# Graph network edge stage: a table chunk moved behind the first units, and DMA issues reordered

## The chip, the cores and the metric

The kernel runs on one core of a Trainium2 chip. The metric is the device time of one execution in microseconds (us). An instruction stream runs on each engine: TensorE (PE, with its weight loads PEld), VectorE (DVE), ScalarE (ACT), GpSimd (POOL) and SyncE (SP, which only waits and issues DMAs).

## The reference, cut to what matters

1250 nodes with 512 features, 40000 edges sorted by destination, two layers. The first layer takes nearly all the time. It works edge by edge:

```
h        = relu(layernorm(x))
pre      = [h[src], h[dst], edge_attr] @ W1 + b1        # 40000 x 1088 @ 1088 x 512
messages = mish(mish(pre) @ W2 + b2)                     # 40000 x 512 @ 512 x 512
agg      = segment_sum(messages, dst)                    # 1250 x 512
u        = mish([h, agg] @ W3 + b3)
x        = x + layernorm(h + u @ W4 + b4) * gamma + beta
```

The second layer is a low-rank product, `h @ U * s @ Vt`, and a sum over the neighbours with the weight of each edge, then bias, relu and residual. The kernel turns that sum into a product with a weighted adjacency matrix M of 1250 x 1250, which it builds in the edge stage of layer one, while it passes over the edges anyway.

## The kernel before, in words

**Prologue.** `h` is transposed and split in a high and a low part (nTh, nTl), so that three products in fast arithmetic give one of full precision. Two tables are made from it in ten chunks of 128 nodes: A = h @ W1[0:512], stored to A_tab, and B = h @ W1[512:1024] + b1, stored as a high and a low half to Bh_tab and Bl_tab. A chunk of B is 12 matmuls on PE (line 723) into one of three banks pB, then on DVE `store_b`: the bias is added (L464), the high half cast (L466), the low half subtracted (L468); SP stores both (`save_b`, L805 and L806). B's ten chunks are the last PE work of the prologue; DVE does `store_b` of them between the first preparations of the edge stage.

**Edge stage.** The edges come in 79 groups of 512. A group has four units: in the first half of the work a unit is a quarter of the 512 hidden features for all 512 edges, in the second half it is a quarter of the edges. Five programs, one for each engine, are written by hand as a loop over slots. In slot s, PE does the first product of unit s+5 (`gathered`: four transposes of gathered rows, L1137; `products`: two matmuls, L1145 and L1147), the second product of unit s (`msg`, 12 matmuls, L1158) and two small ones for M (L1168, L1169); after every fourth slot (s mod 4 = 2) eight matmuls sum the messages of a group by destination (L1181). Units 0 to 3 are done ahead of the slots in four banks (bp0, bp1, pm, bs); the last of them, bs, shares its memory with bank 2 of pB. ACT does exponentials and logarithms of mish (L1217 to L1223 for the first half, L1237 to L1245 for the second); DVE does the square (`square`, L1321), the product and the cast (`pre`, L1331 and L1337), the message (L1344), the bias copy (`bias`, L1350) and the one-hot matrices. Each wait is on a semaphore, and each engine takes its instructions in the written order.

**POOL.** In slot s it subtracts the low half of unit s+4 (`low`, hTl, L1063), and issues DMAs: four indirect gathers for each group (xg, from A_tab, tiles t = 0 to 3, L1050), two that add the summed messages into agg_tab (`accumulate`, L1077) and two that add 128 x 160 pieces into M_tab (`adjacency`, halves 0 and 1, L1088). The tables GATHER_AHEAD and ADJ_LAG say in which slot of four each is issued. Before, tile 0 of a group comes in a slot with s mod 4 = 2, tile 1 with 3, tile 2 with 0 and tile 3 with 1, two slots ahead of its use by PE (s mod 4 = 3 in `gathered`, unit s+5, j = 0, which waits for all four). Each add waits for the landing of the one before it.

**SP.** It loads, per group, the source indices (idx, `indices`, L970), the edge features (ea, L978), the destinations (db, L983), the rows of B in the group's window (`window_rows`, L957 and L958, which needs the products of the group two before) and a copy within the core (`window_copy`, L962). Between the loads of groups 2 and 3 it writes zeros over M_tab in ten DMAs of 640 KB (`zero_m`, L370). POOL's first add into M waits until all ten have landed (semaphore q_zlate, "e_zlate" in the listings).

Of the kernel before, what the change touches and what calls it, by code (L numbers as in the profile page):

```python
# [26 lines left out]
P = 128  # L27
# [188 lines left out]
def gnn_two_layers(nc, x, src_idx, dst_rows, src_cols, dst_cols, eaT, ew_cols, W1, b1, W2, b2, W3, b3, W4, b4,  # L216
# [39 lines left out]
    with ctx:  # L256
# [128 lines left out]
        with st:  # L385
# [70 lines left out]
            def store_b(e, c):  # L456
# [7 lines left out]
                e.tensor_tensor(tb[i][:], pB[i][:, :], b1b[:], ALU.add).then_inc(c_tb, 1)  # L464
                e.wait_ge(c_tb, 3 * c + 1)
                e.tensor_copy(tbh[i][:], tb[i][:]).then_inc(c_tb, 1)  # L466
                e.wait_ge(c_tb, 3 * c + 2)
                e.tensor_tensor(tbl[i][:], tb[i][:], tbh[i][:], ALU.subtract).then_inc(c_tb, 1)  # L468
# [238 lines left out]

            @prologue.on("tensor")
            def _(e):
                e.wait_ge(c_g.sem, 4)  # L710

                def table(c, half, bank):

                    n = 0
                    for a, w in ((nTh, w1h), (nTl, w1h), (nTh, w1l)):
                        if c == 0 and a is nTh and w is w1h:
                            e.wait_ge(*((c_w1h, 1) if half else (c_v.sem, v["w1h"])))
                        if c == 0 and w is w1l:
                            e.wait_ge(c_v.sem, v["w1l", half])
                        if half == 0 and a is nTl:  # L720
                            e.wait_ge(c_lo, c + 1)
                        for k in range(KC):
                            last = e.matmul(bank[:, :], a[:, k, c * P:(c + 1) * P], w[:, half * KC + k, :],
                                            start=n == 0, stop=n == 3 * KC - 1)
                            n += 1
                    return last

                def table_a(c):

                    e.wait_ge(c_hi, c + 1)  # L730
                    if c >= 2:
                        e.wait_ge(c_ta, c - 1)
                    table(c, 0, pA[c % 2]).then_inc(c_A, 1)

                def table_b(c):

                    if c >= TB:
                        e.wait_ge(c_tb, 3 * (c - TB) + 1)
                    table(c, 1, pB[c % TB]).then_inc(c_B, 1)
# [13 lines left out]
                for c in range(NCH):  # L753
                    table_b(c)
# [84 lines left out]
def edge_narrow(work, scope, sem, k):  # L839
# [9 lines left out]
    b_stored, store_b, save_b, q_b2, c_ta, c_tb = (  # L849
        k[n] for n in ("b_stored", "store_b", "save_b", "q_b2", "c_ta", "c_tb"))  # L850
# [26 lines left out]
    with st:  # L877
# [87 lines left out]
        def _(e):  # L965
# [49 lines left out]
            for i in range(3):  # L1015
                zero_m(e, i, q_zlate)
# [1473 lines left out]
```

## Time and profile before

| | us |
|---|---|
| median of 3 runs (1515.99 to 1518.47) | 1516.13 |
| the profiled execution | 1518.77 |
| its span, first to last instruction | 1517.1 |
| PE busy | 1489.8 |
| DVE busy | 1411.0 |
| ACT busy | 1302.0 |
| POOL busy | 1079.7 |

How to read a profile's rows. In a timeline a row has the start from the span's first instruction, the duration, the engine (with q for its queue's own instructions), the line, the operation, output<-inputs, the shape, how many instructions are merged in the row, and in brackets the idle time of the engine ahead of it with what ended that. In the windows view a row gives the busy time and the number of instructions of each engine in a stretch, then the granted clock of TensorE (1.00 is 2.4 GHz, 0.50 is 1.2 GHz), the busy share of the DMA engines and the rate they moved. In the waits view a row says who waited for what, total us, times, longest.

### The profile page before, as it was taken

The numbers are of one execution on the slowest core, as the hardware profiler recorded it, in microseconds if no ns is written. First come the engines' busy times: TensorE is split into PE (matmuls) and PEld (weight loads), VectorE is DVE, ScalarE is ACT, GpSimd is POOL, SyncE is SP. The second block draws the span as 40 slices with busy tenths as digits, with TensorE's granted clock in tenths as the row PEclk, the third lists the DMA queues.
The fourth block names the chain that finished last, engine by engine and source line by source line (L and its number), as shares of the span: only waits on it lengthen the run. The fifth ranks groups of instructions, "written<-read, shape, count | busy, mean of one in ns | idle before, by whom it ended". The sixth has DMA issues, their size and how long they took to land.

```text
span 1517.1 us, 33370 instructions
## 1 busy us (share of the span) xinstructions
PE 1489.8 (98%) x7862; PEld 1167.1 (77%) x7862; DVE 1411.0 (93%) x2920; ACT 1302.0 (86%) x2510; POOL 1079.7 (71%) x978
## 2 busy tenths in 40 slices
PE   7989999999999999999999999999999999999998
PEld 6767777777777777777777777777777777777885
DVE  7888999999999999999999999999999999996676
ACT  5088999999999999999999999999999999996562
POOL 1266888888888888887888888888878888863320
PEclk9999999999999999999999999999999999999999
DMA  8784555455455545444554545454455555554773
GB/s 288 269 280 107 122 123 125 112 131 116 118 122 123 122 115 129 116 118 118 125 118 115 125 123 121 118 125 118 115 123 123 123 117 126 115 135 102 176 166 148
DMA packets 124756, 205.10 MB, mean 135 GB/s; under 512 B 31641, under 2 KB 57369, under 8 KB 124720
## 3 DMA queue, kind: packets, MB, share of 16 engines
q0 software_dynamic: 58528, 112.91, 34.5%
q1 hardware_dynamic: 65840, 91.24, 19.3%
q10 hardware_dynamic: 352, 0.52, 0.1%
q8 instruction: 16, 0.26, 0.1%
q14 instruction: 20, 0.16, 0.0%
HBM read 151.60 MB, written 42.75 MB: 128 GB/s over the span
## 4 chain that ended last, share of the span: by engine, by line
PE 82%; DVE 5%; issue 4%; DMA 4%; POOL 2%; ACT 1%; POOLq 1%; DVEq 0%; SPq 0%; ACTq 0%
PE bm L1158 49%; PE bp L1137 7%; PE bp L1145 5%; PE bs L1181 4%; PE bp L1147 4%; DMA xg<-A_tab,idx 2%; PE pm L1169 2%; PE po L2146 2%; PE pu L336 2%; PE pu L2124 2%; PE pm L1168 1%; POOL hTl L1063 1%; DMA A_tab<-ta 1%; DVE bm L1350 1%; PE pu L2191 1%
## 5 line engine op out<-in xcount | busy, mean ns | idle before, releaser
L1063 POOL TENSOR_TENSOR hTl<-tp,hTh 128x512 fp32r<-128x512 f32 (+1 forms) x314 | 413.0, 1315 | 204.0 <-DVE khl L1357 203.2
L1158 PE MATMUL bm<-W2h,hTh 128*128 128x512 f32 x1252 | 498.3, 398 | 1.2 <-DVE bm L1350 0.8
L1158 PE MATMUL bm<-W2l,hTh 128*128 128x512 f32 x1252 | 496.7, 397 | 0.0
L1158 PE MATMUL bm<-W2h,hTl 128*128 128x512 f32 x1252 | 494.6, 395 | 0.0
L1050 POOL DMA_INDIRECT xg<-A_tab,idx x305 | 321.6, 1054 | 65.3 <-issue 37.7
L1158 PEld LDWEIGHTS bm<-W2h,hTh 128*128 128x128 f32 x1252 | 235.4, 188 | 71.0 <-DVE bm L1350 15.8
L1158 PEld LDWEIGHTS bm<-W2l,hTh 128*128 128x128 f32 x1252 | 235.4, 188 | 57.4
L1158 PEld LDWEIGHTS bm<-W2h,hTl 128*128 128x128 f32 x1252 | 235.5, 188 | 53.7
L1217 ACT ACTIVATE rp<-bp 128x512 f32<-128x512 f32 (+1 forms) x314 | 183.7, 585 | 107.1 <-PE bp L1147 77.3
L1321 DVE SCALAR_TENSOR_TENSOR rp<-rp 128x512 f32<-128x512 f32 (+1 forms) x314 | 214.8, 684 | 36.9 <-ACT rp L1217 17.5
L1331 DVE SCALAR_TENSOR_TENSOR tp<-rp,bp 128x512 f32<-128x512 f32 (+1 forms) x314 | 211.6, 674 | 4.7 <-ACT rp L1223 2.4
L1344 DVE SCALAR_TENSOR_TENSOR tm<-rm,bm 128x512 f32<-128x512 f32 x313 | 210.1, 671 | 3.4 <-ACT rm L1245 3.4
L1350 DVE COPY bm<-b2b 128x512 f32<-128x512 f32 x309 | 210.2, 680 | 0.0
L1220 ACT ACTIVATE rp<-rp 128x512 f32<-128x512 f32 (+1 forms) x314 | 195.5, 623 | 8.8 <-DVE rp L1321 3.0
L1241 ACT ACTIVATE rm<-rm 128x512 f32<-128x512 f32 x313 | 198.0, 633 | 5.0
L1245 ACT ACTIVATE rm<-rm 128x512 f32<-128x512 f32 x313 | 195.2, 624 | 0.1
L1243 ACT ACTIVATE rm<-rm 128x512 f32<-128x512 f32 x313 | 195.1, 623 | 0.1
L1223 ACT ACTIVATE rp<-rp 128x512 f32<-128x512 f32 (+1 forms) x314 | 194.1, 618 | 0.1
L1237 ACT ACTIVATE rm<-bm 128x512 f32<-128x512 f32 x313 | 185.5, 593 | 1.9 <-DVE tm L1344 1.8
L1137 PEld LDWEIGHTS bp<-ident_r,xg 128*128 128x128 f32 (+1 forms) x1244 | 123.8, 141 | 75.3 <-issue 38.0
L1077 POOL DMA_DIRECT2D agg_tab<-ev x157 | 157.1, 1001 | 25.8 <-DMA agg_tab<-ev 16.0
L1088 POOL DMA_DIRECT2D M_tab<-mev x157 | 164.3, 1047 | 10.4 <-issue 9.5
(248 smaller groups left out, 2306.6 us busy)
## 6 DMA issues: line engine op xcount, KB each, us to landing
ea<-in_eaT SPq DMA_DIRECT2D x156, 128.0 KB
M_tab<-mev POOLq DMA_DIRECT2D x157, 80.0 KB, 5.7
agg_tab<-ev POOLq DMA_DIRECT2D x157, 64.0 KB, 2.5
db<-in_dst_rows SPq DMA_DIRECT2D x78, 128.0 KB
M<-M SPq DMA_DIRECT2D x76, 128.0 KB
M_tab<-zero SPq DMA_DIRECT2D x10, 640.0 KB
xg<-A_tab,idx POOLq DMA_INDIRECT x313
eaW<-Bh_tab SPq DMA_DIRECT2D x77, 64.0 KB
```

What stands on the lines that cost most here:

```text
L1050: e.indirect_dma_start(out=xg[p][0:r, t, :].bitcast(F32), out_offset=None, in_=A_d, in_offset=bass.IndirectOffsetOnAxis(ap=idx[p][0:r, t:t ...
L1063: e.tensor_tensor(hTl[p][:, j, 0:w], pick(u, start_t, tp)[:, 0:w], hTh[p][:, j, 0:w], ALU.subtract)\
L1137: e.matmul(bank[:, t * P:t * P + r].bitcast(F32R), xg[p][0:r, t, j * P:(j + 1) * P], ident_r[0:r, 0:r], start=t == 0, stop=False, is_trans ...
L1158: last = e.matmul(bank[0:r, :], a[p][:, c, j * P:j * P + r], w[:, c, :], start=False, stop=c == KC - 1 and w is W2l, skip_group_check=True)
L1220: e.activation(t, t, ACT.Ln, bias=1.0, scale=0.5 / (SQ * SQ)).then_inc(a_pre, 1)
L1241: e.activation(t, t, ACT.Square, bias=SQ, scale=SQ).then_inc(a_msg, 1)
L1243: e.activation(t, t, ACT.Ln, bias=0.5, scale=0.5 / (SQ * SQ)).then_inc(a_msg, 1)
L1245: e.activation(t, t, ACT.Exp, scale=-1.0).then_inc(a_msg, 1)
L1321: e.scalar_tensor_tensor(t, t, 2.0 * SQ, t, ALU.add, ALU.mult).then_inc(v_sq, 1)
L1331: e.scalar_tensor_tensor(t, pick(u, start_r, rp)[:, 0:w], 1.0, pick(u, start_bank, bp)[:, 0:w], ALU.subtract, ALU.mult).then_inc(v_pre, 2 ...
L1344: e.scalar_tensor_tensor(tm[m.const % MBUF][0:r, :], rm[m.const % 2][0:r, :], 1.0, bm[m.j][0:r, :], ALU.subtract, ALU.mult).then_inc(v_msg, 1)
L1350: e.tensor_copy(bm[m.j][:, :], b2b[:]).then_inc(v_bias, 1)
```

## The change

1. B's tenth chunk (c = 9) leaves the prologue on PE and stands behind the products of units 0 to 3 (`table_b(e, NCH - 1)`). PE's wait for the add of chunk 8 (bank bs) now stands only ahead of unit 3.
2. On DVE, `store_b` of that chunk goes behind the four `pre` steps of units 0 to 3. Its sum is written to ta[0] instead of tb[0] (after a wait for the stores of A), and the square of unit 4 stands between its add and its cast. The bias copies into banks 2 and 3 follow it instead of standing among the first squares. The wait for all stores of B moves from the start of the slots to message 2.
3. POOL waits for c_B = 10 (the tenth chunk's matmuls) ahead of the low halves of units 1 to 3.
4. POOL issues tile 3 of a gather behind tile 2, in the same slot (s mod 4 = 0). Half 1 of the adds into M moves from there to the next slot (s mod 4 = 1), behind the add into agg_tab. The two first adds into M both stand in slot 9 (before: slots 6 and 8), one behind the other.
5. SP: the ten zero DMAs of M move behind the loads of group 3 (three of them) and behind the window rows of group 4 (seven).

```diff
@@ store_b
-                e.tensor_tensor(tb[i][:], pB[i][:, :], b1b[:], ALU.add).then_inc(c_tb, 1)
+                total = tb[i] if c < NCH - 1 else ta[0]
+                if c == NCH - 1:
+                    a_stored(e)
+                e.tensor_tensor(total[:], pB[i][:, :], b1b[:], ALU.add).then_inc(c_tb, 1)
+                if between:
+                    between()
...
@@ tables
-    GATHER_AHEAD = {2: (10, (0,)), 3: (9, (1,)), 0: (8, (2,)), 1: (7, (3,))}
+    GATHER_AHEAD = {2: (10, (0,)), 3: (9, (1,)), 0: (8, (2, 3))}
...
-    ADJ_LAG = {2: (6, 0), 0: (8, 1)}
+    ADJ_LAG = {2: (6, 0), 1: (9, 1)}
@@ SP
             b_stored(e)
             window_rows(At(None, 8))
+            window_copy(At(None, 8))
+            loads(At(None, 12))
             for i in range(3):
                 zero_m(e, i, q_zlate)
-            window_copy(At(None, 8))
-            indices(At(None, 12))
-            for i in range(3, 5):
+            indices(At(None, 16))
+            features(At(None, 16))
+            targets(At(None, 16))
+            window_rows(At(None, 16))
+            for i in range(3, NCH):
                 zero_m(e, i, q_zlate)
...
+            window_copy(At(None, 16))
+            loads(At(None, 20))
@@ PE
-            e.wait_ge(c_tb, 3 * (NCH - 2) + 1)
             for j in range(SUB):
+                if j == SUB - 1:
+                    e.wait_ge(c_tb, 3 * (NCH - 2) + 1)
                 gathered(At(None, j))
             for j in range(SUB):
                 products(At(None, j))
+            table_b(e, NCH - 1)
@@ POOL, low and adjacency
                 if first(u) and j:
                     e.wait_ge(a_high, j)
+                    e.wait_ge(c_B, NCH)
...
+                    u = s + -lag
+                    if u.has(4 * FULL) and not (half == 0 and u.reg is None and u.const == 0):
+                        if half == 1 and u.reg is None and u.const == 0:
                             e.wait_ge(q_zlate, 16 * NCH)
-                        adjacency(s + -lag, half)
+                            adjacency(u, 0)
+                        adjacency(u, half)
@@ DVE
-            square(u[0])
-            square(u[1])
-            biases(2)
-            square(u[2])
-            biases(3)
+            for j in range(3):
+                square(u[j])
             pre(u[0], 0)
             pre(u[0], 1)
             square(u[3])
             for j in range(1, SUB):
                 pre(u[j], 0)
-            square(u[4])
-            b_stored(e)
+            store_b(e, NCH - 1, lambda: square(u[4]))
+            biases(2)
+            biases(3)
```

The same work stays in the other branch of the program (general graphs), which these inputs do not take.

PE at the end of the prologue, before: chunk 9 into pB, then units 0 to 3 (bp, bp, pm, bs), and then unit 4 (names in brackets are the semaphores waited for).

```order
L723 MATMUL pB<-w1h,nTh 128x512 [waits c_tb]
L723 MATMUL pB<-w1h,nTh 128x512 x3
L723 MATMUL pB<-w1h,nTl 128x512 x4
L723 MATMUL pB<-w1l,nTh 128x512 x4
L138 TENSOR_LOAD wide_i [waits c_v]
L138 ISA x2
L139 COMPARE_AND_BRANCH
L1137 MATMUL bp<-ident_r,xg 128x128 [waits e_ga0,c_tb]
```

The same place after:

```order
L138 TENSOR_LOAD wide_i [waits c_v]
L138 ISA x2
L139 COMPARE_AND_BRANCH
L1142 MATMUL bp<-ident_r,xg 128x128 [waits e_ga0]
L1142 MATMUL bp<-ident_r,xg 128x128 x7
L1142 MATMUL pm<-ident_r,xg 128x128 x4
L1142 MATMUL bs<-ident_r,xg 128x128 [waits c_tb]
L1142 MATMUL bs<-ident_r,xg 128x128 x3
L1150 MATMUL bp<-M_0,eaW_0 128x512 [waits e_ealow,e_win0]
```

The wait for chunk 8's add has moved to the fourth unit, and chunk 9's matmuls stand behind the eight that begin with L1150 (there as L724).

POOL in the loop, before, the two slots s mod 4 = 0 and 1:

```order
L1063 TENSOR_TENSOR hTl<-tp,hTh 128x512 [waits v_adj]
L1050 DMA xg<-A_tab,idx 128x512
L1082 ISA
L1082 TENSOR_LOAD base_i
L1082 ISA x2
L953 REGISTER_ALU
L1088 ISA [waits e_adjq]
L1088 DMA M_tab<-mev 128x160
L1062 REGISTER_ALU
L1063 TENSOR_TENSOR hTl<-tp,hTh 128x512 [waits v_adj]
L1050 DMA xg<-A_tab,idx 128x512
```

The same two slots after:

```order
L1067 TENSOR_TENSOR hTl<-tp,hTh 128x512 [waits v_adj]
L1053 DMA xg<-A_tab,idx 128x512 x2
L1066 REGISTER_ALU
L1067 TENSOR_TENSOR hTl<-tp,hTh 128x512 [waits v_adj]
L1072 ISA
L1072 TENSOR_LOAD base_i
L1072 ISA x2
L1077 ISA
L958 ISA [waits e_ev]
L1081 ISA [waits e_acc]
L1081 DMA agg_tab<-ev 32x512
```

Tile 3 stands one subtraction and one add earlier; the add into agg_tab (which waits for DVE's e_ev) now follows the subtraction directly, and the add into M comes behind it.

SP after, from the loads of group 4 on (M_0, eaW_0: even groups):

```order
L975 DMA idx<-in_src_idx 128x4 [waits e_ga0]
L983 DMA ea<-in_eaT 64x512 [waits e_ealow]
L983 DMA ea<-in_eaT 64x512
L988 DMA db<-in_dst_rows 64x512
L993 TENSOR_LOAD base_i
L993 ISA x2
L962 ISA [waits e_pre]
L962 DMA eaW_0<-Bh_tab 32x512
L963 DMA eaW_0<-Bl_tab 32x512
L370 DMA M_tab<-zero 512x1x320 x7
L967 DMA M_0<-M_0 64x512 [waits e_prep]
```

The copy of group 4 (L967) and all of group 5's loads stand behind seven zero DMAs, which themselves wait for unit 11's products (e_pre).

## Rows read from the trace of the kernel before

**Rows 1.** The page: busy time (share) and instructions of each engine.

```profile
PE 1489.8 (98%) x7862; PEld 1167.1 (77%) x7862; DVE 1411.0 (93%) x2920; ACT 1302.0 (86%) x2510; POOL 1079.7 (71%) x978
```

**Rows 2.** Timeline of PE in the loop: sums by destination, one transpose group behind.

```profile
132.27 1.06 PE L1181 MATMUL bs<-tm,oh 128*32 128x512 f32 x8
...
715.57 0.52 PE L1137 MATMUL bp<-ident_r,xg 128*128 128x128 f32 x4 [0.31 <-DMA xg<-A_tab,idx]
...
780.82 1.06 PE L1181 MATMUL bs<-tm,oh 128*32 128x512 f32 x8
...
797.37 1.06 PE L1181 MATMUL bs<-tm,oh 128*32 128x512 f32 x8
...
1362.37 1.06 PE L1181 MATMUL bs<-tm,oh 128*32 128x512 f32 x8
```

**Rows 3.** Waits between 132 and 1362 us: total us, times, longest.

```profile
PE bp L1137 <- DMA xg<-A_tab,idx: 3.4, 7, 0.6
```

**Rows 4.** Timeline of POOL in the loop.

```profile
711.90 1.07 POOL L1050 DMA_INDIRECT xg<-A_tab,idx  x1 [0.16 <-DVE ev L1372]
...
725.98 1.01 POOL L1088 DMA_DIRECT2D M_tab<-mev  x1
...
728.49 1.06 POOL L1050 DMA_INDIRECT xg<-A_tab,idx  x1 [0.16 <-issue]
...
731.72 1.29 POOL L1063 TENSOR_TENSOR hTl<-tp,hTh 128x512 fp32r<-128x512 f32 x1 [1.21 <-DVE khl L1357]
```

**Rows 5.** Timelines at the start of the edge stage: ACT's queue, then PE.

```profile
69.88 0.37 ACTq L958 DMA_DIRECT2D eaW<-Bl_tab  x1
...
74.64 0.46 PE L1145 MATMUL bp<-M,eaW 128*128 128x512 f32 x1
```

**Rows 6.** The same stretch: DVE, POOL, DVE, PE.

```profile
74.24 0.43 DVE L466 CAST tbh<-tb 128x512 fp32r<-128x512 f32 x1
...
77.22 0.69 DVE L1408 COPY bm<-b2b 128x512 f32<-128x512 f32 x1
...
83.44 3.01 POOL L1063 TENSOR_TENSOR hTl<-tm,hTh 128x512 fp32r<-128x512 f32 x2
...
84.61 0.69 DVE L1321 SCALAR_TENSOR_TENSOR rp<-rp 128x512 f32<-128x512 f32 x1 [1.18 <-ACT rp L1217]
...
86.86 0.69 DVE L1331 SCALAR_TENSOR_TENSOR tp<-rp,bp 128x512 f32<-128x512 f32 x1 [1.56 <-ACT rp L1223]
...
87.60 0.53 PE L1137 MATMUL bp<-ident_r,xg 128*128 128x128 f32 x4
```

**Rows 7.** The page's DMA issues: count, KB each, median us to landing.

```profile
M_tab<-mev POOLq DMA_DIRECT2D x157, 80.0 KB, 5.7
agg_tab<-ev POOLq DMA_DIRECT2D x157, 64.0 KB, 2.5
```

**Rows 8.** Timelines of PE and POOL around group 3's first unit.

```profile
108.05 0.49 PE L1137 MATMUL bp<-ident_r,xg 128*128 128x128 f32 x4
...
112.00 1.07 PE L1181 MATMUL bs<-tm,oh 128*32 128x512 f32 x8
115.23 0.64 PE L1137 MATMUL bp<-ident_r,xg 128*128 128x128 f32 x4 [2.16 <-DMA xg<-A_tab,idx]
...
120.62 0.49 PE L1137 MATMUL bp<-ident_r,xg 128*128 128x128 f32 x4
...
109.11 0.97 POOL L1050 DMA_INDIRECT xg<-A_tab,idx  x1 [0.15 <-issue]
```

**Rows 9.** Windows: busy time by engine, granted clock, DMA share, GB/s.

```profile
104.00:108.00 4.00, 4.00 (x23) 3.34 (x22) 4.00 (x9) 3.97 (x8) 2.62 (x3) 1.00 1.05 362
...
115.50:118.70 3.20, 3.20 (x10) 2.61 (x10) 1.12 (x3) 1.75 (x4) 0.38 (x1) 0.50 0.44 93
```

**Rows 10.** Timeline of POOL at the end of the edge stage.

```profile
1389.21 0.88 POOL L1088 DMA_DIRECT2D M_tab<-mev  x1 [0.43 <-issue]
...
1392.69 0.88 POOL L1088 DMA_DIRECT2D M_tab<-mev  x1 [0.84 <-DMA M_tab<-mev]
```

More of the change, by code:

```diff
@@ L454, in b_stored, with store_b @@
                     e.wait_ge(q_sb[i], 32 * len(range(i, n, TB)))
-            def store_b(e, c):
+            def store_b(e, c, between=None):
                 i = c % TB
@@ L706, in _, with table, table_b @@
                 store_a(e, 9)
+            def table(e, c, half, bank):
+                n = 0
+                for a, w in ((nTh, w1h), (nTl, w1h), (nTh, w1l)):
+                    if c == 0 and a is nTh and w is w1h:
+                        e.wait_ge(*((c_w1h, 1) if half else (c_v.sem, v["w1h"])))
+                    if c == 0 and w is w1l:
+                        e.wait_ge(c_v.sem, v["w1l", half])
+                    if half == 0 and a is nTl:
+                        e.wait_ge(c_lo, c + 1)
+                    for k in range(KC):
+                        last = e.matmul(bank[:, :], a[:, k, c * P:(c + 1) * P], w[:, half * KC + k, :],
+                                        start=n == 0, stop=n == 3 * KC - 1)
+                        n += 1
+                return last
+            def table_b(e, c):
+                if c >= TB:
+                    e.wait_ge(c_tb, 3 * (c - TB) + 1)
+                table(e, c, 1, pB[c % TB]).then_inc(c_B, 1)
             @prologue.on("tensor")
@@ L710, in _ @@
                 e.wait_ge(c_g.sem, 4)
[L712 to L726, printed above, removed]
                 def table_a(c):
@@ L732, in table_a @@
                         e.wait_ge(c_ta, c - 1)
[L733 to L739, printed above, removed]
+                    table(e, c, 0, pA[c % 2]).then_inc(c_A, 1)
                 for c in range(NCH):
@@ L752, in _ @@
                 table_a(NCH - 1)
-                for c in range(NCH):
-                    table_b(c)
+                for c in range(NCH - 1):
+                    table_b(e, c)
             @prologue.on("sync")
@@ L1112, in step @@
                     lag, half = ADJ_LAG[s.j]
-                    if (s + -lag).has(4 * FULL):
-                        if half == 0 and s.reg is None and s.const == lag:
-                            e.wait_ge(q_z, 16 * ZERO_DMAS)
+                    u = s + -lag
+                    if u.has(4 * FULL) and not (half == 0 and u.reg is None and u.const == 0):
+                        if half == 1 and u.reg is None and u.const == 0:
                             e.wait_ge(q_zlate, 16 * NCH)
-                        adjacency(s + -lag, half)
+                            adjacency(u, 0)
+                        adjacency(u, half)
                 if q.j == 3 and q.has(4 * FULL):
@@ L1342, in msg @@
                 wait(e, s_seg, m.group(1, -1))
+                if m.reg is None and m.const == 2:
+                    b_stored(e)
                 e.wait_ge(a_msg, m.val(4, 4))
@@ L1408, in biases @@
                 e.tensor_copy(bm[j][:, :], b2b[:]).then_inc(v_bias, 1)
-            for c in range(NCH):
+            for c in range(NCH - 1):
                 store_b(e, c)
@@ L1453, in edge_general @@
         k[n] for n in ("q_z", "load_w3", "load_ag", "split_w3x", "xpart", "s_fin", "s_agg"))
-    load_v3, zero_m, settled, store_b, save_b = (
-        k[n] for n in ("load_v3", "zero_m", "settled", "store_b", "save_b"))
+    load_v3, zero_m, settled, store_b, save_b, table_b = (
+        k[n] for n in ("load_v3", "zero_m", "settled", "store_b", "save_b", "table_b"))
     st, sb, ps = scope()
@@ L1616, in _ @@
         def _(e):
+            table_b(e, NCH - 1)
             program("tensor", e)
```

18 lines of the change are left out of this document (5 added, 13 removed).

## The prediction

> **What bounds the kernel now.** I read the page first. PE is busy for 1489.8 of 1517.1 us, DVE for 1411.0 and POOL for 1079.7 [rows 1], and most of the chain that ended last is PE's matmuls. A PE this full can only be helped in two ways: less work on it, which the change doesn't bring (it moves 12 matmuls and removes none), or fewer stops. So I looked for stops on PE in the timeline, and for what ended them.
>
> In the loop, four slots with one sum by destination take 797.37 - 780.82 = 16.55 us where nothing stops PE [rows 2]. That is 1.0 for the sum and 3.89 for a slot. From the sum at 132.27 to that at 1362.37 there are 74 such periods: 1230.10 us, where 74 free ones would take 1224.7. PE loses 5.4 us in all this time. The waits view puts 3.4 of it on seven waits for a gather [rows 3]; one of the seven is at 715.57. The gather it waited for is the fourth tile, issued at 711.90 [rows 4]; so it lands at most 3.7 us after its issue, and in a free period it arrives with next to nothing to spare.
>
> Ahead of the loop PE stops twice. At the start of the edge stage it has no work until ACT and DVE have led the first units through mish. And at group 3's first unit it waits 2.16 us for a gather, issued at 109.11, that took 6.1 us and not 3.7, since the zeros of M fill the DMA engines then (362 GB/s at 104 to 108) [rows 8, 9]. After that stop the granted clock is 0.50 (1.2 GHz) for 3.2 us [rows 9].
>
> **1. The start (the tenth chunk behind units 0 to 3).** PE's work up to chunk 8 stays as it is; what goes is chunk 9's 12 matmuls, 2.8 us, between chunk 8 and unit 0. The first product of unit 0 is at 74.64 [rows 5]. It could start when the window's rows of B are there: the last is issued at 69.88 [rows 5], and the nearest row of such a size, 64 KB, lands in 2.5 [rows 7], so 72.4. That moves the first products forward by 74.64 - 72.4 = 2.2 us. ACT works through its four units without a pause of note; behind it POOL's low halves end at 86.45, and PE reaches slot 1 at 87.60 [rows 6]. All of this would come 2.2 earlier. Chunk 9 itself (74.3 to 77.1) fits in PE's gap before unit 4, and POOL's new wait for it is over well before ACT's casts.
>
> But DVE now has more between unit 3 and slot 0. The add (0.69) fits in its idle 1.18 ahead of unit 4's square [rows 6]. Behind the square, at 85.30 - 2.2 = 83.1, come cast (0.43, as at 74.24), subtraction and two bias copies (0.69, as at 77.22, of which about 0.1 overlaps with the next): 0.45 + 0.65 + 0.6 + 0.6 = 2.3 [rows 6], so unit 4's `pre` starts at 85.4 and not at 86.86 - 2.2 = 84.66 [rows 6]. PE's slot 1 waits for it. Of the 2.2, 1.5 are left. Bounds: 2.2 if DVE's tail is covered, and -1.2 if PE, which now has several gaps of 0.7 to 0.9 us among the first products of slot 0, gets the half clock in slot 1 (3.2 us at half cost 1.6) and a further 1.1 is lost on DVE. I take 1.5, because ACT and DVE rows are the densest evidence.
>
> **2. Group 3's gather (zeros later, tile 3 earlier).** From the sum at 112.00 to slot 8 at 120.62 PE takes 8.62 us where 1.0 + 3.89 = 4.89 would do [rows 8]: 3.7 lost, stop and half clock together. After the change only three zeros (2 MB, 6 us) follow group 3's loads, at about 99 to 106, and tile 3 is issued one slot earlier, near 105.6. Even at 6.1 it lands by 111.7, when PE wants it at 111.4; at the free 3.7, by 109.3. The zeros end early in its flight, so I take the second: +3.7, bounds 3 and 3.7. What is late next is DVE, which has hardly any idle in slots 3 to 6; nothing of that is touched.
>
> **3. The loop.** In the loop tile 3 is issued where half 1 of the add into M stood (725.98), plus 0.3 for two gathers in a row, so at 726.3 and not 728.49: over 2 us earlier, against a lateness of 0.3 to 0.6 [rows 2 to 4]. These late gathers follow hiccups of POOL of 0.7 us, which stay, and are covered then. Of the 5.4 us I take 4.6; bounds 3.4 to 5.4 if it acts.
> What it adds: the add into agg_tab now follows the low half directly and waits for DVE's sum (I estimate under 0.5 us, since the one in front of 711.90 was over at the end of the low half), then the add into M. Both are done a microsecond ahead of the next low half, which has 1.21 us of idle ahead of it [rows 4]. So this is nothing on the path.
>
> **4. Groups 4 and 5 (seven zeros late, two adds at once).** The price of part 2. The seven zeros wait for unit 11's products, in slot 6, which PE starts at 108.05 - 1.5 = 106.55 [rows 8]. SP issues from 108.3. Seven times 0.655 MB and four gathers of 0.26 MB are 5.6 MB; at 362 GB/s [rows 9] that is 15.6 us, at 0.9 of it 17.3, and with 2 us for start and landing the last zero is in at 126 to 128. POOL reaches its first add into M in slot 9. PE starts slots 7, 9 and 11 at 111.4, 119.2 and 128.0; POOL's low half of a slot starts 3.5 later than PE's slot (in slot 5, 109.11 - 1.45 against 108.05 - 3.89), so 122.7, and after it (1.29 + 0.16) and the add into agg (1.05) POOL stands at the zeros' semaphore at 125.3. It waits for 1 to 2.5 us. Then half 1 waits for half 0's landing, at most 3.5 us [rows 10], where before two gathers and adds filled this place. By 131 it goes on with unit 14's low half, and unit 15's, with a gather and an add between, ends at about 136. PE's slot 12, from 131.9, wants it in its eleventh matmul at 135.1. That is about 1 us; with a mishap of the two other things that come at 128 (group 4's copy and its gather) I take 1.3. Bounds 0 and 7 (zeros at 131, then the half clock).
> The Trainium skill, "DMA: Bandwidth & Descriptors", section "Queues, rings and completion order", says that a DMA engine consumes the descriptors of one ring in the order of the ring. By that rule group 4's copy, issued by SP behind seven zeros, cannot land before them, 127 to 129, while PE wants it at 128.3; the rule speaks for a stop of up to 1 us here, which is inside the bounds; no row of before has a load behind so many zeros.
>
> **The sum.** 1.5 + 3.7 + 4.6 - 1.3 = 8.5 us, from the profiled execution's 1518.77 to 1510.3. The plain runs lie 2.6 below it (1516.13), and so may have fewer of the hiccups in part 3; I give back 0.7. Forecast for the median: 1516.13 - 8.5 + 0.7 = 1508.3.
>
> **The rivals.**
> A. The late zeros decide. If the seven zeros and what is behind them land at 131 or later, then PE stops in slot 11 for the copy by about 3 us, and in slot 12 for POOL by 2 more, and the half clock adds 1.7. For it: gathers took 6.1 beside zeros, and everything in part 4 meets within a microsecond. Against it: 362 GB/s was kept up for long. Price 5.5 more than forecast: 1513.8.
> B. The loop gains nothing. If plain runs have no hiccups of POOL, part 3 falls to about 0.6. For it: the gap of 2.6 between profiled and plain. Against it: the seven waits are a property of the gather's spare time, which is near nothing in the plain runs too. Time 1512.
> C. The other side: slower. Half 1 of the add into M now stands one slot (4.3 us) ahead of half 0 of the next group, which waits for its landing; before it was two slots. It decides from a landing of some 7 us: POOL's wait of 2.7 then exceeds its idle (1.21 and 0.6) and the slack of its low half to PE. For it: the page gives 5.7 us for such an add [rows 7], and it adds to 160 columns of 128 rows. Against it: one that was waited for landed within 3.5 [rows 10]. With 0.3 us on each of 76 groups it would cost 23 us: 1531. The skill's same page, section "Anatomy of one DMA — SWDGE (gpsimd) path", gives 2.0 us plus the bytes at 436 GB/s; by it (an estimate, 2.2 us for 80 KB) the pairing costs nothing, and this rival would fall out; the rows show more than that.
> D. The start doesn't gain: DVE's tail and a half clock in slot 1 cost what the earlier products bring, and DVE's lag goes on to slots 3 and 4. Time 1510.5.
>
> **The numbers.** Forecast 0.55 (its own range 1505.5 to 1511); A 0.15, B 0.11, C 0.06, D 0.08; the rest 0.05, on either side. A measurement can tell 0.2%, 3.0 us, so faster means below 1513.1. Forecast, D, most of B and a third of A are faster: 0.78. Within: two thirds of A, a part of B and of the rest, 0.15. Slower: C and a mishap in part 4 beyond its bound, 0.07. The range that leaves out 2 in 10: 1504 to 1514.
>
> **What would show it.** Part 1: the first product of unit 0 near 72.4, slot 1 at about 86.1, DVE without idle between the add's square and unit 4's `pre`. Part 2: no stop of PE at slot 7, and no half clock near 112 to 119. Part 3: no wait for a gather in the loop, every period at 16.55. Part 4: POOL's idle ahead of the first add into M, its low half of unit 15 later than PE's slot 12 by about 1 us. It is wrong if PE stops for several us in slots 9 to 12, if POOL waits for its own adds in every group, or if periods of the loop grow above 16.6.

## The result, and the profile after

| | before | after |
|---|---|---|
| median of 4 runs, side by side | 1516.79 (1515.99 to 1518.47) | 1528.18 (1525.91 to 1530.70) |
| the profiled execution | 1518.77 | 1528.38 |
| its span | 1517.1 | 1526.7 |
| its mean granted clock | 0.997 | 0.995 |

The changed kernel is slower: ratio 1.0075, 95% interval 1.0061 to 1.0089, 11.4 us. The forecast was 1508.3, its range 1504 to 1514.

The page of the changed kernel, where [rows 1] stands for before:

```profile
PE 1494.7 (98%) x7862; PEld 1169.3 (77%) x7862; DVE 1429.5 (94%) x2920; ACT 1304.4 (85%) x2510; POOL 1071.6 (70%) x978
```

The same number of instructions on every engine. But DVE is busy 18.5 us longer, and PE 4.9: some instructions take longer than they did.

To see where, I set the starts of the same matmuls in the two traces beside each other (after minus before): the first product -1.6, slot 2 +3.3, slot 8 (behind the stop that went) -1.6, slot 16 and on +1.9, the loop's last sum 1365.09 - 1362.37 = +2.7, and the end of the span +9.6. So the largest loss, 6.9 us, comes behind the loop, for which the prediction has no term. Now the parts in the order of the prediction.

**The start.** Timelines of PE, DVE and POOL of the changed kernel, to be read against [rows 5, 6], and the window of the low clock.

```profile
73.08 0.50 PE L1150 MATMUL bp<-M,eaW 128*128 128x512 f32 x1 [1.86 <-DMA eaW<-Bl_tab]
...
88.10 0.75 PE L1142 MATMUL bp<-ident_r,xg 128*128 128x128 f32 x4 [2.26 <-DVE tp L1338]
...
83.08 2.11 DVE L1328 SCALAR_TENSOR_TENSOR rp<-rp 128x512 f32<-128x512 f32 x1 [0.58 <-ACT rp L1224]
...
87.36 0.68 DVE L1338 SCALAR_TENSOR_TENSOR tp<-rp,bp 128x512 f32<-128x512 f32 x1
...
82.12 2.51 POOL L1067 TENSOR_TENSOR hTl<-tm,hTh 128x512 fp32r<-128x512 f32 x2
...
87.50:94.30 6.80, 6.20 (x17) 4.97 (x18) 6.01 (x11) 5.12 (x9) 2.68 (x2) 0.50 0.48 161
```

The first product is 1.56 us earlier. Then the square of unit 4 takes 2.11 us where it took 0.69. It starts while POOL is in its last two low halves (82.12 to 84.63), and it ends at 85.19, 0.56 behind them, where its own length is 0.69: it stood nearly still until POOL was through. Unit 4's `pre` is at 87.36 instead of 86.86, PE waits 2.26 us for it, and the granted clock is 0.50 (1.2 GHz) for 6.8 us from 87.5 on.

That it is the square is not the rule. In the profiles of e1, e2 and e12, whose start is the same, the square takes 0.69, POOL's two low halves take 3.00 beside it instead of 2.51, and the cast of chunk 9 behind it is long, 1.51 us where 0.43 is usual. DVE and POOL of e1:

```profile
82.38 0.69 DVE L1329 SCALAR_TENSOR_TENSOR rp<-rp 128x512 f32<-128x512 f32 x1 [0.58 <-ACT rp L1225]
82.99 1.51 DVE L471 CAST tbh<-ta 128x512 fp32r<-128x512 f32 x1
...
81.21 3.00 POOL L1067 TENSOR_TENSOR hTl<-tm,hTh 128x512 fp32r<-128x512 f32 x2
```

So one DVE instruction of this stretch is held by the low halves each time. From the square's start to unit 4's `pre` it is 4.28 us in the changed kernel and 3.95 in e1.

The low clock moved too. In the profiles of the nine kernels with the start of before it comes once, for 3.4 or 6.8 us, and ends ahead of slot 1 (before: 0.50 from 81.3 to 84.7). In four of the five with the moved start it lies on slot 1, whose matmuls of 512 columns then take 0.63 us and not 0.40, from 86.1 at the earliest to 94.3 at the latest (3.4 us in e1 and e12, 6.8 in e2 and here; here another 3.4 us from 73.9 on come on top). The fifth is e8, see there.

The Trainium skill, "SBUF — State Buffer", section "Who interferes with whom", says that a DVE instruction with two inputs in SBUF contends with a GpSimd instruction that reads SBUF. The square multiplies rp with itself, both from SBUF, and the low half reads hTh there; the trace agrees, with 2.11 us for 0.69. The square was held through both low halves, although the second of them began only at 83.37.

**Slot 7 and slots 11 to 13.** PE and POOL of the changed kernel, against [rows 8]:

```profile
114.11 1.06 PE L1186 MATMUL bs<-tm,oh 128*32 128x512 f32 x8
115.10 0.53 PE L1142 MATMUL bp<-ident_r,xg 128*128 128x128 f32 x4
...
130.73 1.07 PE L1186 MATMUL bs<-tm,oh 128*32 128x512 f32 x8
133.46 0.50 PE L1142 MATMUL bp<-ident_r,xg 128*128 128x128 f32 x4 [1.66 <-DMA xg<-A_tab,idx]
...
139.51 0.50 PE L1163 MATMUL bm<-W2h,hTh 128*128 128x512 f32 x1 [1.15 <-DVE bm L1359]
...
125.82 0.95 POOL L1053 DMA_INDIRECT xg<-A_tab,idx  x1 [0.30 <-issue]
...
130.76 0.94 POOL L1092 DMA_DIRECT2D M_tab<-mev  x1 [0.63 <-issue]
135.44 0.85 POOL L1092 DMA_DIRECT2D M_tab<-mev  x1 [3.73 <-DMA M_tab<-mev]
```

The stop ahead of slot 7 is gone. One group later the fourth gather, issued at 125.82 behind the seven zeros, lets PE wait until 133.3 (7.5 us in flight), and POOL waits 3.73 us between its two first adds. For the zeros themselves it does not wait: the last of them has landed at 129.5, and POOL comes to its first add at 130.76.

**The loop.** PE's sums at either end, the row of the one-hot in the groups view of DVE between 150 and 1360 us (count, then total and mean ns), and one of the three groups in which it is worst (DVE, POOL):

```profile
150.82 1.06 PE L1186 MATMUL bs<-tm,oh 128*32 128x512 f32 x8
...
1365.09 1.06 PE L1186 MATMUL bs<-tm,oh 128*32 128x512 f32 x8
```

```profile
L1318 DVE TENSOR_TENSOR oh<-iota_w,drel 128x128 f32<-128x128 f32 x73 | 47.1, 646 | 0.0
```

```profile
616.77 2.00 DVE L1318 TENSOR_TENSOR oh<-iota_w,drel 128x128 f32<-128x128 f32 x1
...
614.94 0.90 POOL L1081 DMA_DIRECT2D agg_tab<-ev  x1 [2.26 <-issue]
616.36 0.93 POOL L1092 DMA_DIRECT2D M_tab<-mev  x1 [0.52 <-issue]
616.99 1.63 POOL L1067 TENSOR_TENSOR hTl<-tp,hTh 128x512 fp32r<-128x512 f32 x1
```

The seven waits for a gather [rows 3] are gone, none is left. But the 73 periods take 1365.09 - 150.82 = 1214.27 us, and before it were 1213.43. The one-hot, which also reads two tensors of SBUF, has a mean of 646 ns; before, the same row has 405. POOL's low half in that slot (s mod 4 = 2) now stands right behind the moved add into M, and the one-hot meets it (616.77 and 616.99). Three times, 250 us apart, POOL hesitates (2.26 us ahead of the add into agg_tab, with nothing to wait for), the one-hot takes 2.0 us, and the period is 17.7 to 17.8 instead of 16.55.

**Behind the loop.** POOL, ACT and PE of the changed kernel, and two windows (the last number is GB/s):

```profile
1365.14 0.86 POOL L1092 DMA_DIRECT2D M_tab<-mev  x1 [0.56 <-issue]
...
1372.95 0.87 POOL L1092 DMA_DIRECT2D M_tab<-mev  x1 [5.63 <-ACT mev L1259]
1373.55 1.56 POOL L1067 TENSOR_TENSOR hTl<-tp,hTh 128x512 fp32r<-128x512 f32 x1
...
1372.31 0.44 ACT L1259 ACTIVATE mev<-pm 128x320 f32<-128x320 f32 x1 [1.24 <-DMA M_tab<-mev]
...
1375.17 0.50 PE L1163 MATMUL bm<-W2h,hTh 128*128 128x512 f32 x1 [2.73 <-POOL hTl L1067]
...
1401.80 1.97 PE L2120 MATMUL pt<-ident,ag 128*128 128x128 f32 x8 [2.31 <-issue]
...
1365.00:1372.30 7.30, 7.30 (x39) 5.04 (x38) 7.16 (x18) 5.16 (x13) 2.18 (x2) 1.00 0.81 261
...
1401.60:1405.00 3.40, 3.21 (x12) 2.92 (x13) 1.94 (x3) 1.80 (x3) 1.55 (x2) 0.51 0.98 333
```

And before, POOL and ACT at the same place:

```profile
1363.84 0.88 POOL L1088 DMA_DIRECT2D M_tab<-mev  x1
...
1368.23 0.44 ACT L1252 ACTIVATE mev<-pm 128x320 f32<-128x320 f32 x1
```

The row at 1363.84 is half 0 of a group, as is the one at 1372.95 of the changed kernel; the half 1 ahead of it had been issued at 1355.89, long ago. In the changed kernel half 1 is issued only at 1365.14. It lands at 1372.3, 7.1 us later. The DMA engines move 261 GB/s in that time, where the loop has some 120, since the loads of the next stage have begun. Two engines wait for that landing. POOL's half 0 waits for all adds before it. ACT's copy of pm into mev waits too, because it overwrites the buffer that the add reads. The bracket of POOL's row names ACT's copy, but that copy lasts until 1372.75, and POOL's own queue had ended its wait by then, at the same moment as ACT's (the view of line 958, POOL and ACT, 1370 to 1373 us):

```profile
L958 POOLq EVENT_SEMAPHORE  x1: 17/17/17, 1372.3 to 1372.3; - x1
L958 ACTq EVENT_SEMAPHORE  x1: 17/17/17, 1372.3 to 1372.3; - x1
```

POOL's low half is queued behind half 0, and PE waits 2.73 us for the low half. From this sum to the next PE takes 18.33 us (1365.09 to 1383.42) instead of 15.34.

That is 3.0 us of the 6.9. The other 3.9 come at another place, 2.4 in a second stop and 1.5 behind it. PE's stop of 2.31 us ahead of the node stage is ended by "issue", so by nothing that the profile shows, and its own queue is in the branch to the next part of the program (line 139), after and before:

```profile
L139 PEldq COMPARE_BRANCH  x1: 3602/3602/3602, 1398.1 to 1398.1; - x1
...
L139 PEldq COMPARE_BRANCH  x1: 183/183/183, 1391.6 to 1391.6; - x1
```

The branch takes 3.60 us where it took 0.18, and the clock is 0.51 (1.2 GHz) for 3.4 us behind it. It is long too in e1 (3.40), e2 (2.52) and e8 (3.66), and under 0.5 us in all others, e3 and e4 among them, which have half 1 where the changed kernel has it. All four with a long branch have the moved start, but so has e12 with 0.42. What makes it long, no run tells.

### The profile page after: what moved, and what is told of

Its sections match the earlier page's. It is cut to its first block, busy times and chain, and to the rows that moved or that the text cites. A ratio compares the mean times of both kernels' runs of the same rounds, so it can differ in the third digit from the quotient of the medians.

```text
span 1526.7 us, 33278 instructions
## 1 busy us (share of the span) xinstructions
PE 1494.7 (98%) x7862; PEld 1169.3 (77%) x7862; DVE 1429.5 (94%) x2920; ACT 1304.4 (85%) x2510; POOL 1071.6 (70%) x978
## 4 chain that ended last, share of the span: by engine, by line
PE 88%; DVE 5%; issue 2%; ACT 2%; DMA 2%; POOL 0%; DVEq 0%; POOLq 0%; ACTq 0%; SPq 0%
PE bm L1163 52%; PE bp L1142 7%; PE bp L1150 6%; PE bs L1186 5%; PE bp L1152 4%; PE pm L1174 2%; PE pu L336 2%; PE po L2154 2%; PE pu L2132 2%; PE pA L724 2%; PE pm L1173 1%; PE pu L2199 1%; PE pB L724 1%; DMA M_tab<-mev 1%; DVE bm L1359 1%
## 5 line engine op out<-in xcount | busy, mean ns | idle before, releaser
L1067 POOL TENSOR_TENSOR hTl<-tp,hTh 128x512 fp32r<-128x512 f32 (+1 forms) x314 | 421.5, 1342 | 110.2 <-DVE khl L1366 107.0
L1053 POOL DMA_INDIRECT xg<-A_tab,idx x305 | 326.8, 1071 | 81.5 <-issue 54.1
L1328 DVE SCALAR_TENSOR_TENSOR rp<-rp 128x512 f32<-128x512 f32 (+1 forms) x314 | 217.1, 691 | 23.4 <-ACT rp L1224 18.5
L1081 POOL DMA_DIRECT2D agg_tab<-ev x157 | 150.4, 958 | 75.4 <-DVE ev L1381 59.5
L1092 POOL DMA_DIRECT2D M_tab<-mev x157 | 150.5, 958 | 49.7 <-issue 36.5
```

The lines of the kernel that those rows point to most:

```text
L1053: e.indirect_dma_start(out=xg[p][0:r, t, :].bitcast(F32), out_offset=None, in_=A_d, in_offset=bass.IndirectOffsetOnAxis(ap=idx[p][0:r, t:t ...
L1067: e.tensor_tensor(hTl[p][:, j, 0:w], pick(u, start_t, tp)[:, 0:w], hTh[p][:, j, 0:w], ALU.subtract)\
L1328: e.scalar_tensor_tensor(t, t, 2.0 * SQ, t, ALU.add, ALU.mult).then_inc(v_sq, 1)
```

## The experiments

Twelve kernels, each timed beside the kernel before. Times are medians; "over before" is the ratio of the two with its interval.

| | what it is | median | before beside it | over before |
|---|---|---|---|---|
| e1 | after, half 1 in its old slot behind the loop | 1520.41 | 1517.38 | 1.0016 (1.0006 to 1.0025) |
| e2 | after, one-hot a slot later | 1540.69 | 1517.38 | 1.0160 (1.0142 to 1.0178) |
| e3 | after, start of before | 1525.90 | 1517.38 | 1.0055 (1.0041 to 1.0069) |
| e4 | before, half 1 a slot later | 1523.44 | 1517.38 | 1.0040 (1.0026 to 1.0055) |
| e5 | before, zeros moved | 1520.25 | 1517.24 | 1.0019 (1.0010 to 1.0028) |
| e6 | before, half 1 a slot earlier | 1522.40 | 1517.24 | 1.0031 (1.0022 to 1.0040) |
| e7 | e6, zeros five and five | 1522.74 | 1517.24 | 1.0034 (1.0022 to 1.0047) |
| e8 | before, start moved, square last | 1524.42 | 1517.24 | 1.0041 (1.0027 to 1.0055) |
| e9 | before, gathers paired | 1517.02 | 1517.05 | 0.9999 (0.9990 to 1.0008) |
| e10 | before, half 1 a slot later in the loop alone | 1517.92 | 1517.05 | 1.0007 (0.9998 to 1.0016) |
| e11 | e10, one-hot ahead of so and khl | 1515.06 | 1517.05 | 0.9986 (0.9977 to 0.9995) |
| e12 | e1, one-hot ahead of so and khl | 1518.51 | 1517.05 | 1.0011 (1.0002 to 1.0020) |

### e1: half 1 back behind the loop

```diff
-                if s.j in ADJ_LAG:
-                    lag, half = ADJ_LAG[s.j]
+                adj = {2: (6, 0), 0: (8, 1)} if s.reg is None and s.const >= LOOP1 else ADJ_LAG
+                if s.j in adj:
+                    lag, half = adj[s.j]
```

> The changed kernel, but from slot 296 on (behind the loop) half 1 of the adds into M stands in the slot with s mod 4 = 0 again, one slot earlier, as before. Theory T1 (the tail loses because half 1, issued one slot later at 1365.14, lands at 1372.2 and ACT's copy of mev, POOL's next add and low half wait behind it): the time falls by about 6.5 us against the changed kernel, to 1521.5, and PE has no 2.3 us stop in front of the node stage. Rival (the tail loses because everything there stands at another place against the big loads, whatever POOL issues when): no change, 1528.

Measured 1520.41, 7.8 below the changed kernel. POOL and ACT of e1:

```profile
1364.65 0.88 POOL L1092 DMA_DIRECT2D M_tab<-mev  x1
...
1369.03 0.44 ACT L1260 ACTIVATE mev<-pm 128x320 f32<-128x320 f32 x1
```

ACT's copy stands there without a wait, the sums are 15.35 apart again (1363.16 to 1378.51). So T1 holds for the stop behind the loop. Its second part fails: PE still stops ahead of the node stage, for 1.17 us, in the long branch. And not all of the 7.8 is the tail's. Between the two profiles (7.5 us apart) 1.9 us lie ahead of the loop's last sum, where the low clock falls otherwise (in e1 3.4 us at the start and 3.4 us from 132.7 on); 3.0 are the stop; and 2.6 lie at the branch and behind it. e4 and e10 give a cleaner price.

### e2: the one-hot one slot later

```diff
-    ONE_LAG = 2
+    ONE_LAG = 3
```

> The changed kernel, but DVE's one-hot matrix (oh) stands one slot later (s mod 4 = 3 and not 2). Theory T4 (in the changed kernel POOL's low half of the slot with s mod 4 = 2 comes 0.1 to 0.2 us later against DVE, since the add into M now stands right ahead of it, and the one-hot, which reads two tensors of SBUF, waits for it: 0.53 to 0.67 us instead of 0.40 in each group, 2.0 us in three): oh is at 0.40 again, the three periods of 17.7 are gone, and the loop gains 4 to 5 us, 1523.5. Rival (the longer periods come from POOL waiting for its own adds): oh 0.40, periods as they are, 1528.

Measured 1540.69, 12.5 above the changed kernel: both expectations missed. The periods of 17.7 are still there, and each is followed by two to four of 18.0. POOL of e2 in one of them:

```profile
389.27 2.45 POOL L1053 DMA_INDIRECT xg<-A_tab,idx  x1 [0.17 <-issue]
391.71 0.98 POOL L1092 DMA_DIRECT2D M_tab<-mev  x1
392.34 1.68 POOL L1067 TENSOR_TENSOR hTl<-tp,hTh 128x512 fp32r<-128x512 f32 x1
```

The issue of a gather takes 2.45 us (1.05 is usual) and the one-hot then 1.67 (392.51). Once POOL is late, the new place makes it late again in the next group. So the meeting of the two engines sets the period, but a later place of the one-hot does not avoid it.

### e3: the start of before

```diff
-            store_b(e, NCH - 1, lambda: square(u[4]))
-            biases(2)
-            biases(3)
+            square(u[4])
+            b_stored(e)
```

and so on for PE's chunk 9, POOL's wait for c_B and the order of the squares, all as before.

> The changed kernel with the start of before: chunk 9 in front of unit 0's products, square of unit 4 behind the four preparations. Theory T2 (square of unit 4, 2.11 us beside POOL's low halves, and the half clock of 6.8 us behind it cost more than the earlier first product brings): slot 2 starts 3 us earlier, and since the next slots give a part back, the end is 1 to 2 us earlier, 1527. Rival (the start is a gain that stays, 1.5 us): 1529.5.

Measured 1525.90, 2.3 below the changed kernel. The intervals of the two ratios overlap (1.0061 to 1.0089 and 1.0041 to 1.0069), so the size is rough and even the sign only likely; it is T2's. Part of the 2.3 can also be the long branch, which e3 does not have.

### e4: half 1 later, alone

```diff
-    ADJ_LAG = {2: (6, 0), 0: (8, 1)}
+    ADJ_LAG = {2: (6, 0), 1: (9, 1)}
```

> The kernel before, with half 1 of the adds into M moved one slot later alone (ADJ_LAG 1: (9, 1)); gathers, zeros and start as before. Theory T1: the tail is 6 to 7 us longer, and the loop keeps its late gathers (5 us), so 1516.8 + 6.5 = 1523.3. Rival (the tail's loss comes with the paired gathers or the shift of the start): as before, 1517.

Measured 1523.44, 6.1 above before, as T1 has it. From the loop's last sum to the next PE takes 21.27 us: the same stop, 2.69 us, and 6.8 us of low clock behind it, which the changed kernel's profile does not have there. What I had not expected is the loop: there is no late gather although the gathers are as before, its 73 periods take 1214.11, and three of them 17.75 to 17.82. Tile 3 comes out of the shadow of the add into M as soon as that add leaves the slot ahead.

### e5: the zeros, alone

```diff
+            window_copy(At(None, 8))
+            loads(At(None, 12))
             for i in range(3):
                 zero_m(e, i, q_zlate)
...
+            window_rows(At(None, 16))
+            for i in range(3, NCH):
+                zero_m(e, i, q_zlate)
```

and group 0's two first adds both in slot 9.

> The kernel before, with the zeros of M moved as in the change (three behind group 3's loads, seven behind group 4's rows) and group 0's two first adds both in slot 9; everything else as before. Theory T3 (the stop of 3.7 us ahead of slot 7 goes, and about as much comes back in slots 11 to 13, where a gather takes 7.5 us beside the zeros and POOL waits for its add): unit 20 within 0.5 us of before, loop and tail as before, 1517.4. Rival (the loss behind slot 11 in the changed kernel came from the other edits): the 3.7 us stay, 1513.7.

Measured 1520.25, 3.0 above before (1.5 to 4.2 by the interval): neither. The stop ahead of slot 7 did not go, since the gather's last tile keeps its old slot here, and behind slot 11 PE now stops too. PE of e5:

```profile
110.72 1.07 PE L1181 MATMUL bs<-tm,oh 128*32 128x512 f32 x8
112.90 0.50 PE L1137 MATMUL bp<-ident_r,xg 128*128 128x128 f32 x4 [1.11 <-DMA xg<-A_tab,idx]
...
131.01 0.51 PE L1137 MATMUL bp<-ident_r,xg 128*128 128x128 f32 x4 [1.46 <-DVE tp L1331]
```

### e6 and e7: half 1 earlier, and the zeros in two halves

```diff
-    ADJ_LAG = {2: (6, 0), 0: (8, 1)}
+    ADJ_LAG = {2: (6, 0), 3: (7, 1)}
```

> The kernel before, with half 1 of the adds into M one slot earlier instead of later (lag 7, s mod 4 = 3), behind the second add into agg_tab. If the loop's late gathers come from half 1 standing ahead of the low half in front of tile 3, and the changed kernel's one-hot and tail losses from half 1 standing ahead of the low half of the next slot and late for ACT, then this one has neither: no wait for a gather, oh at 0.40 us, tail as before, 1512.5. Rival (four issues in one slot push the low half of the next into a DVE instruction that reads two tensors of SBUF): periods of 16.6 and more, 1517 or above.

Measured 1522.40, 5.2 above before: the rival. The one-hot is short (0.41), but now the issues of slot 3 press on the next slot. The squares of the loop have a mean of 719 ns (690 before), and 89 of POOL's issues between 150 and 1360 us take over 1.2 us, where 3 did.

```diff
+            window_copy(At(None, 12))
+            indices(At(None, 16))
+            features(At(None, 16))
+            targets(At(None, 16))
+            window_rows(At(None, 16))
             for i in range(5, NCH):
                 zero_m(e, i, q_zlate)
```

> e6 and the zeros of M in two parts of five: the first five where they stand before, the last five behind group 4's rows; group 0's first adds both in slot 9. If T3's two losses come each from more than 3 MB of zeros in front of a gather, both are gone: no stop ahead of slot 7 and none in slot 11, 3 us less than e6, 1509.5. Rival (five late zeros still hold group 4's gather or POOL's first adds): as e6, 1512.5.

Measured 1522.74, no different from e6. In its profile the sum of group 1 is 2.3 us earlier than e6's (127.50 against 129.82) and the gain is gone by the next one (146.81 against 146.63). What a shorter stop gives at slot 7, slots 11 to 13 take.

### e8: the start alone, the square behind the store

```diff
-            store_b(e, NCH - 1, lambda: square(u[4]))
+            store_b(e, NCH - 1)
+            square(u[4])
```

on a kernel with the change's start and otherwise the code of before.

> The kernel before with the change's start alone, but on DVE the square of unit 4 stands behind the cast and the subtraction of chunk 9 and not in front of them. Theory T2 in its form with the port (the square, which reads SBUF alone, waits for POOL's low halves of units 2 and 3, 2.11 us instead of 0.69): cast and subtraction fill part of that time, unit 4's preparation comes 0.5 to 0.9 us earlier than in the changed kernel, and the time is 0.5 to 1.5 us above before, 1518.4. Rival (the half clock behind the gap of PE costs it whatever the order on DVE): 2.3 us above before, as the changed start costs by e3, 1519.7.

Measured 1524.42, 7.2 above before: neither. PE and SP's queue of e8:

```profile
85.50 0.33 SPq L810 DMA_DIRECT2D Bh_tab<-tbh  x1
...
91.50 2.68 SPq L370 DMA_DIRECT2D M_tab<-zero  x3
94.23 1.40 SPq L967 DMA_DIRECT2D M<-M  x1
...
88.18 0.54 PE L1143 MATMUL bp<-ident_r,xg 128*128 128x128 f32 x4 [2.04 <-DVE tp L1339]
...
99.71 0.50 PE L1151 MATMUL bp<-M,eaW 128*128 128x512 f32 x1 [3.28 <-DMA M<-M]
```

The order on DVE gained nothing: the cast took 0.95 us and the subtraction, which also reads two tensors of SBUF, 1.65 (83.82), so they were held in the square's place, and PE's slot 1 is at 88.18. And chunk 9 is stored only at 85.50, so SP is later with everything behind it: group 2's copy, behind three zeros, makes PE wait 3.28 us at slot 3. In the change the zeros stand behind that copy. So the moved start needs the moved zeros; I had priced the two apart.

### e9: the pairing, alone

```diff
-    GATHER_AHEAD = {2: (10, (0,)), 3: (9, (1,)), 0: (8, (2,)), 1: (7, (3,))}
+    GATHER_AHEAD = {2: (10, (0,)), 3: (9, (1,)), 0: (8, (2, 3))}
```

> The kernel before with the gathers paired alone: tile 3 behind tile 2 in the slot with s mod 4 = 0, half 1 of the add into M behind both, in the same slot. If the pairing is what takes the late gathers away (prediction, part 3), PE waits for no gather in the loop, and with the one-hot where it was against POOL the loop gains 4 to 5 us: 1512.8. Rival (three issues push POOL's next low half 0.9 us back, into a DVE instruction that reads two tensors of SBUF): periods above 16.6, 1518 or more.

Measured 1517.02: no change. The late gathers of the loop are gone, and the 73 periods take 1213.88. In their place stand seven of 17.2. DVE and POOL of e9 in one:

```profile
494.32 1.68 DVE L1321 SCALAR_TENSOR_TENSOR rp<-rp 128x512 f32<-128x512 f32 x1
...
493.68 1.77 POOL L1063 TENSOR_TENSOR hTl<-tp,hTh 128x512 fp32r<-128x512 f32 x1
```

The low half is pushed back by the third issue, and where POOL hesitated (0.63 us ahead of a gather at 490.35), a square waits for it: 1.68 us for 0.69. It is the same collision with another victim.

### e10 and e11: half 1 later in the loop alone, and the one-hot ahead

e10 is e4 with the lines of e1.

> The kernel before with half 1 of the adds into M one slot later in the loop, and in its old slot from slot 296 on. By e4 (6.1 us above before, of it 5 to 6 in the tail) this takes the tail's loss away: 1517.5, with no late gather, but the one-hot at 0.65 us and three periods of 17.7. Rival (the tail loses because the loop's last adds are late too): 1521.

Measured 1517.92, with the loop at 1213.71. Against e4 5.5 us less, by the tail's edit alone: this is the price of the later half 1 there. Then the one-hot:

```diff
+                h = s + -ONE_LAG
+                if h.j == 0 and h.has(MSGS) and not (h.reg is None and h.const <= SUB):
+                    onehot(h)
                 if (s + ADJ_AHEAD).has(MSGS) and not (s.reg is None and s.const == 0):
                     adjacency(s + ADJ_AHEAD)
...
                 if m.has(MSGS):
                     msg(m)
-                h = s + -ONE_LAG
-                if h.j == 0 and h.has(MSGS) and not (h.reg is None and h.const <= SUB):
-                    onehot(h)
```

> e10, and on DVE the one-hot stands ahead of the two matrices for M (so, khl) of its slot instead of at the slot's end. POOL's low half waits for khl or for POOL itself, so the one-hot is over before it. If the collision of the two is what took the loop's gain: one-hot at 0.40 us, no period of 17.7, the loop 4 to 5 us shorter, 1512.8. Rival (as in e2, another order on DVE brings another collision): one-hot short, but casts, squares or gathers long, 1517 or more.

Measured 1515.06, 2.9 below e10, and the fastest kernel here: 2.0 us under before (0.8 to 3.5 by the interval), 13 under the changed one. The one-hot's row in the groups view of DVE, 150 to 1360 us, and PE's sums:

```profile
L1312 DVE TENSOR_TENSOR oh<-iota_w,drel 128x128 f32<-128x128 f32 x73 | 20.2, 277 | 0.0
```

```profile
145.14 1.06 PE L1182 MATMUL bs<-tm,oh 128*32 128x512 f32 x8
...
1356.04 1.06 PE L1182 MATMUL bs<-tm,oh 128*32 128x512 f32 x8
```

277 ns, and 73 periods in 1210.90: 2.8 us shorter than e10's, which is the whole difference of the medians. The mechanism is shown; of the expected 4 to 5 us it gives 2.8, as three periods of 17.0 to 17.1 stay. The step takes the one-hot from 661 ns in e10 to 277, below the 405 of before, so it also takes away what the kernel before lost there.

### e12: the changed kernel with both mendings

The lines of e1 and e11 in the changed kernel.

> The changed kernel with both mendings: half 1 of the adds into M in its old slot from slot 296 on, and the one-hot ahead of so and khl. Sum of e1 (7.8 us below the changed kernel) and the loop's 4 to 5 us: 1516. Against e11 it carries the change's start and its zeros, which by e3 and e5 cost 2 to 3 us. Rival (the shift of the start moves the loop into another collision): 1520.

Measured 1518.51, 9.7 below the changed kernel, 3.5 above e11: the start and the zeros together cost that (and the pairing, which e9 puts at nothing).

## Why the prediction was wrong

**Part 1, the start: +1.5 forecast, about -2 measured (e3, roughly).** The first product came at 73.08 (72.4 forecast; 72.38 in e1), so the window's rows did bound it. That the 2.5 us taken for their landing fit so well is partly luck: the row for it in [rows 7] is the landing of one add, behind the edge stage. The step that failed is DVE's tail, added up from the lengths of free rows at a place where POOL is in its low halves. From the square's start to unit 4's `pre` 3.0 us were forecast, and it is 4.28, with the square at 2.11, or 3.95 in e1 and e12, with the cast at 1.51. [Rows 6] held the warning: the pair of low halves of 3.01 us encloses that very square, and two of them alone take 2.51. One engine had already waited there, for the other; I read the 3.01 as POOL's own length. The low clock in slot 1, which I had only as a bound, came in four of the five profiles with this start, for 3.4 or 6.8 us. And the store of chunk 9, which the step moves on DVE, moves on SP too, with all loads behind it (e8).

**Part 2, slot 7: +3.7 forecast, 1.4 to 3.7 measured.** The stop went. The size was that of one execution. In the profiles of e4, e6, e10 and e11, whose code up to there is that of before, PE waits 1.67, 1.78, 1.71 and 1.32 us. PE of e11:

```profile
110.55 1.07 PE L1182 MATMUL bs<-tm,oh 128*32 128x512 f32 x8
112.94 0.51 PE L1138 MATMUL bp<-ident_r,xg 128*128 128x128 f32 x4 [1.32 <-DMA xg<-A_tab,idx]
```

From this sum to the next one these four take 18.32, 18.45, 19.83 and 17.97 us, against 20.27 in the profile of before and 16.55 in a free period. So the term was 1.4 to 1.9 us in three executions, and 3.3 and 3.7 in e10 and before, where the low clock follows the stop for 3.4 us. The profiled one was 2.6 above the median; I gave back 0.7 for that, and on the loop, where it did not belong. And neither of the two edits removes the stop by itself: it stays with the zeros alone (e5, 1.11) and with the pairing alone (e9, 0.93).

**Part 3, the loop: +4.6 forecast, -0.8 measured.** The mechanism was right, zero late gathers instead of seven. What failed is the sentence "So this is nothing on the path". I asked whether POOL's two adds are over a microsecond ahead of the low half, and did not ask which DVE instructions stand beside that low half. The add moved it onto the one-hot (405 to 646 ns); e11 against e10, where the one-hot goes from 661 to 277, prices the meeting at 2.8 us. And the pairing, to which I gave the gain, isn't needed for it: e4 has no late gather without it.

**Part 4, the late zeros: -1.3 forecast, bounds 0 to 7.** e5 puts the price at 3.0 (1.5 to 4.2), inside the bounds. The gather beside the zeros took 7.5 us and not the 6.1 of before, and POOL waited 3.73 between its adds (3.5 had been the bound for one alone). The wait for the zeros, forecast at 1 to 2.5 us, did not come, and the stop for group 4's gather (1.66), held for a mishap, did.

**The tail: nothing forecast, 5.5 us measured (e10 against e4).** This is the largest term, and the step that failed is that the forecast put it at nothing: half 1's later place was priced in the loop alone. Rival C named the edit and the wait, half 0 of the next group waiting on POOL for the landing of half 1, and it named the length that decides, some 7 us. It laid this in each group. There no such wait came, since an add of the loop lands within 2.6 to 4.0 us by the updates of its semaphore. It came once, behind the loop, where the add takes 7.1 us beside the loads of the next stage. There ACT's copy waits for the same landing. The 5.7 us of [rows 7] could not tell the two places apart: it is the landing of a single add, at 1404.80, also behind the loop (the view of mev in before, 1400 to 1410 us).

The parts for themselves: tail 5.5, zeros 3.0, start 2.3, loop 0.8, slot 7 -1.4 to -3.7, together 7.9 to 10.2 for the 11.4 measured. They come from single profiles and from medians with intervals of 2 to 3 us, and they do not add exactly. The long branch of PE's queue, 2.3 us of stop with 3.4 us of low clock behind it, has no term of its own here. It may be the rest, or be in part in the start's 2.3; no run changes it alone.

## What to carry to other kernels

When an instruction of GpSimd or VectorE changes its place, set the two engines' rows side by side and mark each pair that reads SBUF with two inputs on one side: a row that is longer than its kind (3.01 for two times 1.25, 646 for 405 ns) is a wait that no bracket shows. When a DMA is moved later, list everything that waits for its landing, on every engine, and look at the place with the slowest landings, which here was not in the loop. Ask of a median in the page how many landings it is made of, and of a stop ended by "issue" what the engine's own queue is doing. And a stop read from one execution is the size of that execution; a row from a second run, or its distance from the median, says how far it can be trusted.

## What the runs showed that I had not expected

- POOL and DVE can fall into a slower beat and stay in it for several groups: in e2 up to four periods in a row of 18.0 us, with gather issues of 2.45 to 2.75 us instead of 1.05.
- A stop of PE of about 2 us was followed by the low clock in one case (2.26 us, then 6.8 us at 0.50) and not in the next (e8: 2.04 us, and the granted clock from 84 to 92 us is 1.00). Behind the loop the same stop was followed by 6.8 us of it in e4 (2.69 us) and by none in the changed kernel (2.73 us).
- Each other place of half 1 of the add into M meets another DVE instruction: in slot 1 the one-hot (e4), in slot 3 squares (e6), and in slot 0 behind three issues, where POOL hesitates, a square (e9).
